# Unit 7 of each gang joins the light units of the top-31 search, its mask made by GpSimd

## The reference

```python
x = x + 0.5 * ffn(layernorm(x), ...)     # 16 experts' q, k, v mixed by the gate, causal attention
x = x + attn(layernorm(x), ...)
x = x + 0.5 * ffn(layernorm(x), ...)

# attn: 16 heads of 16, U = int(5 * log(512)) = 31
scores = einsum('bhqd,bhkd->bhqk', Q, K) / sqrt(D)
thresh = top_k(scores, U)[0][..., -1:]
scores = where(scores < thresh, -inf, scores)
context = einsum('bhqk,bhkd->bhqd', softmax(scores), V)
```

## Time and profile before

| | |
|---|---|
| Median of 3 runs | 4768.65 us (4768.02 to 4772.23) |
| The profiled execution | 4764.82 us |
| Its span, first to last instruction | 4763.0 us |
| Mean granted TensorE clock, share of full speed | 0.929 |
| Instructions profiled | 123642 |

### The profile page before, as it was taken

How to read it: one execution, slowest core, us unless ns; L and a number is a source line. 1 busy time by engine, 2 the same in 40 slices (tenths; PEclk the granted TensorE clock), 3 DMA queues, 4 the chain that set the end, 5 groups by cost and what they waited for, 6 DMA issues and landing times. The chain is left out here.

```text
span 4763.0 us, 123642 instructions
## 1 busy us (share of the span) xinstructions
PE 4148.0 (87%) x33100; PEld 3434.0 (72%) x33100; DVE 4335.3 (91%) x10070; ACT 3972.8 (83%) x10181; POOL 3107.6 (65%) x5079
## 2 busy tenths in 40 slices
PE   5767889898998989898999989999898999987776
PEld 4556777787777777777777777777777777765555
DVE  0199999999999999999999999999999999999980
ACT  2378989898888989898888988889888989888772
POOL 5545676767667676767767676777667677654444
PEclk8888999999999999999999999999999999988888
DMA  3101111111111111111111111211111111110011
GB/s 86 53 21 33 50 53 49 55 50 52 53 51 52 49 55 48 54 51 53 52 49 54 49 55 48 55 49 53 51 51 52 49 55 49 54 38 26 21 30 49
DMA packets 244185, 232.90 MB, mean 49 GB/s; under 512 B 27123, under 2 KB 176628, under 8 KB 243316
## 3 DMA queue, kind: packets, MB, share of 16 engines
q1 hardware_dynamic: 243444, 224.49, 16.5%
HBM read 214.98 MB, written 9.44 MB: 47 GB/s over the span
## 5 line engine op out<-in xcount | busy, mean ns | idle before, releaser
L886 DVE MAX8 M<-W 128x8 f32<-128x512 f32 x2688 | 1735.7, 681 | 56.0
L538 PE MATMUL pQ<-wf_sb,HS 128*128 128x192 f32 x8192 | 1553.7, 347 | 105.2 <-POOL HS L991 104.2
L538 PEld LDWEIGHTS pQ<-wf_sb,HS 128*128 128x128 f32 x8192 | 1445.7, 204 | 154.3 <-issue 78.2
L888 DVE MATCH_REPLACE8 W<-M,W 128x512 f32<-128x512 f32 x1664 | 1115.5, 676 | 0.0
L1028 POOL TENSOR_TENSOR XL<-S,LM 128x512 f32<-128x512 f32 x384 | 446.2, 1162 | 927.2 <-ACT LM L768 889.0
L557 PE MATMUL pST<-ident,S 128*128 128x128 f32 x4096 | 751.7, 284 | 15.8 <-ACT S L756 15.8
L783 ACT ACTIVATE OUT<-S,M 128x512 bf16<-128x512 f32 x1024 | 741.7, 724 | 1.1 <-issue 1.1
L787 ACT ACTIVATE S<-S,M 128x512 f32<-128x512 f32 x1024 | 737.1, 720 | 0.0
L559 PE MATMUL pST<-steep,OUT 128*128 128x128 bf16 x4096 | 735.7, 223 | 0.0
L888 DVE MATCH_REPLACE8 W<-M,S 128x512 f32<-128x512 f32 x1024 | 684.5, 676 | 0.0
L886 DVE MAX8 M<-S 128x8 f32<-128x512 f32 x1024 | 651.7, 678 | 20.0 <-issue 19.0
(11 more groups left out here) (231 smaller groups left out, 6575.5 us busy)
## 6 DMA issues: line engine op xcount, KB each, us to landing
RB<-rows_b SPq DMA_DIRECT2D x384, 256.0 KB, 3.3
RB<-rows_a SPq DMA_DIRECT2D x384, 256.0 KB, 3.3
x_b<-in_x SPq DMA_DIRECT2D x64, 128.0 KB, 2.8
out_y<-y SPq DMA_DIRECT2D x64, 128.0 KB, 1.8
wf_sb<-in_wf SPq DMA_DIRECT2D x4, 768.0 KB, 7.4
rows_b<-rwT_b SPq DMA_DIRECT2D x64, 8.0 KB, 1.3
wof_sb<-in_wof SPq DMA_DIRECT2D x1, 1024.0 KB, 7.3
rows_a<-rwT_a SPq DMA_DIRECT2D x64, 8.0 KB, 1.4
```

The source lines that it names most:

```text
L538: mm = nc.tensor.matmul(pQ[:, 0:QKV], HS[:, k % 2, e, i, :], wf_sb[:, i, at:at + QKV], start=k + e + i == 0, stop=(k, e, i) == (3, 3, 1))
L886: nc.vector.max(m, src[i]).then_inc(s_tk, 1)
L888: nc.vector.match_replace(W[:, i, :], m, src[i], -BIG).then_inc(s_tk, 1)
```

## The change

Unit 7 of each gang is a light unit as well, so that each pair of a gang has one. Units 1, 3 and 5 (`BY_ACT`) keep their way. For unit 7 (`BY_POOL`) the mask is made by GpSimd, with a comparison of S with the 24th value and a multiplication by 2^40 in one instruction, in GpSimd's slot 12, right ahead of the subtraction into XL. It waits for VectorE's third MAX8 of the unit. The count is made by ScalarE in slot 13 (`LCNT`, 7 + 6), with a pass over LM that writes to a spare tile and accumulates into cnt. It stands behind the four exponentials of that slot and ahead of OUT and S. The picking and the threshold of unit 7 are as those of the other light units, in slots 15 and 16. Since there are now two makers of masks, the waits on s_low, s_lr and the new s_lpm and s_lcnt count each kind's units by themselves (`kin`). The loop over windows runs from 0 instead of from 1, with the windows' numbers moved into the constants.

```diff
--- before.py
+++ after.py
@@ -26,7 +26,10 @@
 PASSES = 2 * ROUNDS - 1
 
 GANG = 8
-LIGHT = (1, 3, 5,)
+LIGHT = (1, 3, 5, 7,)
+
+BY_POOL = (7,)
+BY_ACT = tuple(u for u in LIGHT if u not in BY_POOL)
 FOUND = 8 * (ROUNDS - 1)
 ORDER = [(p, i, k) for p in range(GANG // 2) for k in range(PASSES) for i in range(2) if k < PASSES - 2 or 2 * p + i not in LIGHT]
 STEEP = 2.0 ** 80
@@ -51,7 +54,7 @@
 
 SC, EV, TOP, OUTS, GAP, TR, PTE, PV, CT, CTT, CTX = 2, 3, 4, 10, 11, 16, 17, 18, 19, 20, 21
 
-LOW, LCOPY, LTOP, LPICK, LTH = 6, 6, 8, 9, 10
+LOW, LCOPY, LCNT, LTOP, LPICK, LTH = 6, 6, 7, 8, 9, 10
 
 
 AT = {
@@ -141,6 +144,11 @@
             n, c = at
             return n * len(LIGHT) + k, c * len(LIGHT) + k, GANG * c + u
     return None
+
+
+def kin(w, c, u, kind):
+
+    return w.count(SPAN // GANG * len(kind), c // len(LIGHT) * len(kind) + kind.index(u % GANG))
 
 
 def fill(n, w, j):
@@ -193,6 +201,7 @@
         LM = sb("LM", P, 2, T, dtype=BF16)
         XL = sb("XL", P, 2, T)
         below = sb("below", P, T, dtype=BF16)
+        spare = sb("spare", P, T, dtype=BF16)
         lower = sb("lower", P, 1)
         iota = sb("iota", P, 8)
         cnt = sb("cnt", P, 2, 1)
@@ -266,8 +275,8 @@
         s_simsq, s_simps, s_simg, s_simr, s_simn = (sem(n) for n in ("s_simsq", "s_simps", "s_simg", "s_simr", "s_simn"))
         s_gexp, s_gadd, s_grec, s_gps, s_sig = (sem(n) for n in ("s_gexp", "s_gadd", "s_grec", "s_gps", "s_sig"))
         s_kb, s_bop, s_bo, s_half = sem("s_kb"), sem("s_bop"), sem("s_bo"), sem("s_half")
-        s_lr, s_low, s_lx, s_ltop, s_lpos, s_lpick, s_lval, s_lth = (
-            sem(n) for n in ("s_lr", "s_low", "s_lx", "s_ltop", "s_lpos", "s_lpick", "s_lval", "s_lth"))
+        s_lr, s_low, s_lpm, s_lcnt, s_lx, s_ltop, s_lpos, s_lpick, s_lval, s_lth = (
+            sem(n) for n in ("s_lr", "s_low", "s_lpm", "s_lcnt", "s_lx", "s_ltop", "s_lpos", "s_lpick", "s_lval", "s_lth"))
         s_sc, s_ev, s_tk, s_gap, s_pt, s_pe, s_pv, s_oc, s_ot, s_o, s_vm = (
             sem(n) for n in ("s_sc", "s_ev", "s_tk", "s_gap", "s_pt", "s_pe", "s_pv", "s_oc",
                              "s_ot", "s_o", "s_vm"))
@@ -288,10 +297,10 @@
             for i in range(FIRST, LOOP[0]):
                 for j in range(SPAN):
                     slot(Window(i, i, i), j)
-            with eng.Fori(LOOP[0] // TURN, (LOOP[1] + 1) // TURN) as i:
+            with eng.Fori(0, (LOOP[1] + 1 - LOOP[0]) // TURN) as i:
                 for a in range(TURN):
                     for j in range(SPAN):
-                        slot(Window(i, LOOP[0] + a, LOOP[1] + 1 - TURN + a, TURN, a), j)
+                        slot(Window(i, LOOP[0] + a, LOOP[1] + 1 - TURN + a, TURN, LOOP[0] + a), j)
             for i in range(LOOP[1] + 1, FINAL + 1):
                 for j in range(SPAN):
                     slot(Window(i, i, i), j)
@@ -742,9 +751,9 @@
                     act.wait_ge(s_bop, 1)
                     nc.scalar.copy(bo_row[:, 1, :], pO[0:1, 0:D]).then_inc(s_bo, 1)
                     act.wait_ge(s_kb, 1)
-                if at := light(w, j, LOW):
+                if (at := light(w, j, LOW)) and at[2] % GANG in BY_ACT:
                     n, c, u = at
-                    wait(act, s_low, n)
+                    wait(act, s_low, kin(w, c, u, BY_ACT))
                     held(act, s_tk, passed(w, u, PASSES - 3))
                     nc.scalar.activation(below[:], S[:, u % RING, :], ACT.Relu, bias=M8[:, u % RING, FOUND - 1:FOUND],
                                          scale=-1.0).then_inc(s_lr, 1)
@@ -760,13 +769,21 @@
                     for h in range(HG):
                         act.wait_ge(s_pt, w.count(SPAN, 4 * c + h + 1))
                         nc.scalar.activation(PTs[:, h, :], pST[h][:], ACT.Exp, scale=-HD ** -0.5).then_inc(s_pe, 1)
-                if at := light(w, j, LOW):
+                if (at := light(w, j, LOW)) and at[2] % GANG in BY_ACT:
                     n, c, u = at
                     wait(act, s_lx, n - 1)
+                    wait(act, s_lcnt, kin(w, c // len(LIGHT) * len(LIGHT), BY_POOL[0], BY_POOL))
                     wait(act, s_lpos, n - 1)
-                    held(act, s_lr, n + 1)
+                    held(act, s_lr, kin(w, c, u, BY_ACT) + 1)
                     nc.scalar.activation(LM[:, c % 2, :], below[:], ACT.Relu, bias=lower[:], scale=-STEEPER,
                                          accum_out=cnt[:, c % 2, :]).then_inc(s_low, 1)
+                if (at := light(w, j, LCNT)) and at[2] % GANG in BY_POOL:
+                    n, c, u = at
+                    wait(act, s_lcnt, kin(w, c, u, BY_POOL))
+                    wait(act, s_lpos, n - 1)
+                    held(act, s_lpm, kin(w, c, u, BY_POOL) + 1)
+                    nc.scalar.activation(spare[:], LM[:, c % 2, :], ACT.Identity, accum_out=cnt[:, c % 2, :]
+                                         ).then_inc(s_lcnt, 1)
                 if at := light(w, j, LTH):
                     n, c, u = at
                     held(act, s_lval, n + 1)
@@ -1023,13 +1040,23 @@
                 if at := light(w, j, LCOPY):
                     n, c, u = at
                     r = u % RING
-                    wait(pool, s_ltop, n - 1)
-                    pool.wait_ge(s_low, n + 1)
+                    if u % GANG in BY_ACT:
+                        wait(pool, s_ltop, n - 1)
+                        pool.wait_ge(s_low, kin(w, c, u, BY_ACT) + 1)
+                    else:
+                        held(pool, s_tk, passed(w, u, PASSES - 3))
+                        nc.gpsimd.tensor_scalar(LM[:, c % 2, :], S[:, r, :], M8[:, r, FOUND - 1:FOUND], LOWER, ALU.is_ge,
+                                                ALU.mult).then_inc(s_lpm, 1)
+                        wait(pool, s_ltop, n - 1)
+                        pool.wait_ge(s_lpm, kin(w, c, u, BY_POOL) + 1)
                     nc.gpsimd.tensor_tensor(XL[:, c % 2, :], S[:, r, :], LM[:, c % 2, :], ALU.subtract).then_inc(s_lx, 1)
                 if at := light(w, j, LPICK):
                     n, c, u = at
                     r = u % RING
-                    held(pool, s_low, n + 1)
+                    if u % GANG in BY_ACT:
+                        held(pool, s_low, kin(w, c, u, BY_ACT) + 1)
+                    else:
+                        held(pool, s_lcnt, kin(w, c, u, BY_POOL) + 1)
                     nc.gpsimd.tensor_scalar(pos[:], cnt[:, c % 2, :], -1.0 / LOWER, -float(TH + 1), ALU.mult, ALU.max).then_inc(s_lpos, 1)
                     wait(pool, s_lval, n)
                     held(pool, s_lpos, n + 1)
```

## The result

The changed kernel takes 4923.74 us (median of 4 runs, 4919.0 to 4926.03) against 4770.34 us of the kernel before (4768.02 to 4772.23): a ratio of 1.032, 95% interval 1.0307 to 1.0333, so 153 us slower. The forecast was 4733 us, in a range of 4710 to 4777; even the slower rival had 4821. The profiled execution's span is 4916.3 us.

A forecast was written before the change was run, and what follows sets the result against it. VectorE was taken to set the pace. Three windows keeping 3.4 us and 13 keeping 2.0 sum to 36 us saved: 4768.65 - 36 = 4733 us, range 4710 to 4777.

The forecast's parts named there:

- the slower rival: GpSimd's mask comes late, ScalarE stands at the count with everything queued behind it: 4817 profiled, 4821 us; chance 0.13.
- What bounds the kernel: Steady stretch 900 to 4100 us: VectorE, busy 98%, sets the pace and everything else keeps up with it.
- VectorE's saving, 54 us: Unit 7 loses a replacement in VectorE's pairs: 0.42 us a gang over 128 gangs, 54 us.
- ScalarE's 0.80 us a gang: ScalarE's count pass over LM plus unit 7's threshold add 0.80 us a gang, 102 us over 128 gangs.
- Does it fit; 18 us of loss: ScalarE's slack of 130 us covers 113 on the mean; uneven slack loses 1.4 of 3.4 us in 13 windows.
- GpSimd's new work, taken to cost no time: Comparison, subtraction and small operations ahead of HS, 3.3 us a gang, 423 us, in an engine 30% idle.
- the cover: TensorE would wait 0.8 us for the later HS, covered by its 9% idle time, 2.9 us a gang.
- The one place that was read: HS starting at 2183.38 on GpSimd: it would end at 2188.1 instead of 2185.8; TensorE takes it at 2187.32.
- It would cost 0.8 us a gang if that cover were gone: TensorE's wait for HS, should its idle time not cover it: 0.8 us a gang; given no chance.
- the text's three signs of being wrong: Count waits microseconds; below's wait stays long while VectorE waits elsewhere; comparison takes over 3 us.
- The rule of the Trainium skill: GpSimd's tight one-input loop at about 1.8 cycles an element puts the comparison near 0.77 us, TensorE's wait 0.4 us.
- The Trainium skill's advice: Plain elementwise work belongs on VectorE, not GpSimd; cited in favour of the slower rival.

The follow-up runs named there:

- dummies of the same kind two slots earlier: Kernel before, plus an unread comparison and subtraction over 512 columns on GpSimd in slot 10 instead of 12: 4771.37 us, 1.0006.
- The late y products: Changed kernel, TensorE's first four of eight products of mixT_a with wof_sb one slot later: 4809.23 us; with the comparison over 8 columns too: 4746.24 us.

## Why the prediction was wrong

- **What bounds the kernel.** VectorE, with waits of 24 us in the stretch: right. But it was read as if the others had reserve, and TensorE's hand-overs were never listed.
- **VectorE's saving, 54 us.** Right: pairs of 8.29 to 8.31 us, 2560 full-width replacements for 2688, 512 MAX8 on XL.
- **ScalarE's 0.80 us a gang.** Right: the count's start to OUT's is 0.61 us (2434.84 to 2435.45), the threshold's share 0.19 (2439.10 to 2439.29). The estimate from the Trainium skill (ScalarE: Activation LUTs, section "What ACT_TABLE_LOAD costs") was the same, and the trace agrees. ScalarE's busy time rose by 113 us against 80 to 100 forecast, 78 of it the count (128 by 0.61).
- **Does it fit; 18 us of loss.** Not contradicted: half of ScalarE's load was worth 5 to 11 us. With comparison and count cut short, 4741 us; with the comparison alone cut short, 4746, and VectorE's waits for Sr_a at 27 us, where 15 to 30 were forecast. The wait for `below` fell under 40 us in the changed kernel (24.4), as forecast, but for another reason: ScalarE spent the time waiting for TensorE (for x1r 76.5 us, 27.7 before; for S 57.3, 11.7 before).
- **GpSimd's new work, taken to cost no time: the step that failed,** in two places. First its price. The comparison was put at the subtraction's 1.16 us; it takes 2.02. By the 92 us that each microsecond of it costs, an estimate for 1.16 us is 4769 + 92 x 0.82 = 4844, still 74 us slower than before. So the price is some 80 of the 191 us between forecast and result, if the line holds between the measured points. Second, and by itself enough for the wrong sign, the cover. The text said that TensorE waits 0.8 us a gang for HS and that its 2.9 us of idle cover that. This idle is made of waits at other places of an ordered list (143.8 us for h_a and 110.6 for rw_b of some 272) and could not be spent at HS: TensorE waited 187.6 us there. The instruction behind HS on GpSimd, mixT_a, was not looked at, although the question "what is queued behind it" had been asked of ScalarE. The one place that was read the earlier trace rows is a gang with mixT_b behind it (2189.27), the hand-over with 3.65 us of reserve; in every second gang it is mixT_a, with 0.48. "It would cost 0.8 us a gang if that cover were gone", 83 to 102 us, is near the loss that the line above gives for the forecast's comparison (4844 less 4733, 111), but it got no chance and was no rival.
- **The slower rival** (4821 us) had the right sign and the wrong mechanism. The count has no idle ahead of it (2434.84, behind four exponentials), and shows no wait in the changed kernel; only with the comparison behind HS did it wait (55 us). None of the text's three signs of being wrong came true: all three asked after ScalarE's count and `below` or after a comparison of over 3 us, none after TensorE.
- **The rule of the Trainium skill** (GPSIMD Engine Reference, section 3.1) gives about 1.8 cycles an element as the best case of a tight one-input loop, an estimate of 0.77 us for 512 columns. The trace does not agree for this operation: alone it took 1.58 us, with the multiplication 2.02. So it does not price this operation. The Trainium skill's advice (same page, section 4.1) to give plain elementwise work to VectorE is not settled by this; dummies of the same kind two slots earlier cost nothing.

What stays open: the 24 us between 4741 and the 4717 that VectorE's saving allows (TensorE still waits 35.5 us for HS there, behind the subtraction), and how the loss divides between mixT and HS in the changed kernel. The late y products gave back 115 us there and 23 us with the short comparison (4769 to 4746), so the two are not additive.

## What to carry to other kernels

Before putting an operation into an engine's ordered list, read for each thing that this engine makes in this slot and the next one how long after its end the taker starts on it. If that reserve is less than the new operation, the taker's idle share elsewhere is no cover, and everything behind it in the taker's list is late. Read it in every kind of gang or tile that the place comes round to, not in one: here two alternate, with 0.48 and 3.65 us. Price the operation from a row of its own kind (operation, types, pointer operand), not from one of its width; if there is none, keep twice the nearest row in the sum, and look at what the time does there.

## What was not expected of the hardware

On GpSimd a comparison with a pointer operand and a multiplication, 128x512, f32 to bf16, takes 2.02 us, the comparison alone 1.58, the subtraction of two inputs of the same width 1.16 (1.04 for the dummies', from f32 to bf16). Over 8 columns the comparison takes 0.34 us. So 504 columns are 1.68 us, 3.3 ns a column, against 2.5 ns with one operation ((1.58 - 0.34) / 504, with the 8-column row of the two operations). One input is dearer than two here.

A wait of TensorE can cost more than its length. Behind the 2.18 us for mixT, the eight matmuls took 3.58 us and not 1.99, at a granted clock of 0.50, that is 1.2 GHz, before it rose again to 2.4 (stretches of the changed kernel; columns as in the earlier trace rows):

```profile
2437.00:2440.00 3.00, 0.82 (x6) 0.55 (x4) 3.00 (x8) 2.88 (x9) 2.80 (x4) 0.97 0.07 24
2440.00:2441.00 1.00, 1.00 (x3) 0.82 (x4) 1.00 (x2) 0.60 (x1) 0.83 (x3) 0.50 0.00 0
...
2442.00:2443.00 1.00, 1.00 (x3) 0.79 (x3) 0.66 (x1) 0.00 (x0) 1.00 (x2) 0.50 0.96 272
2443.00:2444.00 1.00, 1.00 (x10) 0.31 (x8) 0.00 (x0) 0.00 (x0) 1.00 (x1) 0.90 0.38 89
```

It is no general cause of the slowdown: the eight matmuls of job a are that slow in 5 of the stretch's 45 tiles, and the clock's mean over the stretch is 0.96, where it was 0.95 before. The kernel before has more of such places: job b's first half of the y products (eight matmuls a tile) takes 546 ns a matmul in the mean there, and 384 in the changed kernel. At 2473.09 of the kernel before it stands right behind TensorE's wait of 4.08 us for h_a and takes 3.62 us.
